# Pair pass of a graph network: edges cut on a fixed grid of 128-edge cells, first attribute stored turned, four PSUM banks for each product

## The chip, the cores and the metric

The kernel runs on one core of a Trainium2 chip. The time is device microseconds from launch to the last result; three runs gave 6835.71, 6841.29 and 6842.03 us, the median is 6841.29 us.

## The reference

A graph has 6250 nodes with 128 features and 106250 edges, sorted by target node. Four blocks are applied in turn: two attention layers, a normalised graph convolution, a block that uses attributes of each edge, and three graph convolutions. The change is about the third block (`_L2_gnn_ref`), after a layer norm and a ReLU of the node features:

```
pos_e = x_feat[src] + edge_attr
v     = gelu(pos_e @ W1.T + b1) * bases
aggr  = segment_sum(v, dst)
```

`edge_attr` and `bases` are two inputs of 106250 x 128. The kernel uses that (x[src] + attr) W = (x W)[src] + attr W: the rows x W + b lie in a table in DRAM, and each edge needs one gathered row, one product of its attribute and one row of `bases`.

## The kernel before, in words

Nodes lie in 49 blocks of 128. A tile is 128 consecutive edges, taken to belong to one block; edges of a neighbour block in it are masked (their LOCAL number, the target's place in the block, is 128 or more, so no one-hot row has a one for them). There are 880 tiles, 220 groups of 4 (GT). Before, the first tile of a block starts at the block's first edge. `tile_tables` works out on VectorE the tables that say which block and which first edge each tile has, by a chain of small operations in which each waits for the one before. Then GpSimd fetches each tile's window of targets, sources and weights by indirect DMA, and VectorE makes LOCAL, SRC, KEY and others of them. Five passes use these tables. `sort_edges` counts whether any target is smaller than the one before; the counting sort runs only then, and these inputs are sorted.

`pair_pass` has one piece of code for each step of a group, and `pipeline` writes them out for step u = 0, 1, 2, ... with a distance ("late"): a piece with distance d works on group u - d. Every engine runs its own pieces in that order. Before, for group q:

- `gather_rows` (distance 0, GpSimd, line 1033): 4 indirect DMAs, each bringing 128 rows of the table into one of 12 group slots (DEEP); it waits until group q - 12 is summed.
- `fetch` (0, SyncE, L1643 to L1657): loads the 4 tiles' first edges into registers, branches on sorted or not, and issues 4 loads of 128 x 256 (attribute and base side by side, 128 KB) into one of 6 slots (PD).
- `turn_attr` (1, TensorE, L1666): 4 transposes of the attribute into PSUM.
- `copy_attr` (1, ScalarE, L1673): PSUM to SBUF. It waits for `attr_turned` and `pre_done` alone.
- `times_w` (2, TensorE, L1681): 4 products with the weight into one of two banks `pre`.
- `sum_up` (2, VectorE, L1690): adds the gathered rows; it waits for the product, the gathers and a slot of V.
- `gelu` (2, ScalarE, L1694), `times_base` (3, VectorE, L1700).
- `hots` (2, VectorE, L1045): 4 one-hot matrices.
- `products` (4, TensorE, L1714): 4 products that sum the edges by target, into one of two banks `sums`.
- `add` (5, VectorE, L1063): 4 additions to the blocks' accumulators, each waiting for the one before.

`into_pair_pass` ahead of it stores the table, so no gather can start earlier; `two_norms` after it starts behind a barrier. Two attention passes (the L1033 rows with ACC) and the three last convolutions (L1348) also gather through GpSimd.

## Time and profile before

| | |
|---|---|
| median of the runs | 6841.29 us |
| span of the profiled execution | 8166.8 us |
| mean granted TensorE clock in it | 0.779 of full |
| pair pass, first to last gather issued | 5108.4 to 6471.1 us |
| GpSimd busy over the span | 57% |
| TensorE busy over the span | 74% |

The page gives no time of the profiled execution beside its span; that span is 1325.5 us above the median of the runs, so durations and gaps below are of an execution that was a fifth longer than a run. A row of the trace says how often an instruction came, how long one took, and what ended the idle time before it on its engine. The name behind a DMA releaser is a guess where several transfers share a semaphore.

### The profile page before, as it was taken

The numbers are of one execution on the slowest core, as the hardware profiler recorded it, in microseconds if no ns is written. First come the engines' busy times: TensorE is split into PE (matmuls) and PEld (weight loads), VectorE is DVE, ScalarE is ACT, GpSimd is POOL, SyncE is SP. The second block draws the span as 40 slices with busy tenths as digits, with TensorE's granted clock in tenths as the row PEclk, the third lists the DMA queues.
The fourth block names the chain that finished last, engine by engine and source line by source line (L and its number), as shares of the span: only waits on it lengthen the run. The fifth ranks groups of instructions, "written<-read, shape, count | busy, mean of one in ns | idle before, by whom it ended". The sixth has DMA issues, their size and how long they took to land. (4 is left out here: it accounts for less than half of the span.)

```text
span 8166.8 us, 113382 instructions
## 1 busy us (share of the span) xinstructions
PE 6013.4 (74%) x30494; PEld 4713.9 (58%) x30494; DVE 3761.8 (46%) x13003; ACT 2160.8 (26%) x7007; POOL 4622.4 (57%) x4391
## 2 busy tenths in 40 slices
PE   3788878646766888876686887455555689989898
PEld 2666766535665666655575887355555544544545
DVE  5344443148973444311688335344555543333333
ACT  3222222228852222222697002111111220000000
POOL 2555555567865555555786552666666436366363
PEclk8666666768976666677898999677777789999999
DMA  5566654356642333323444664444444557867777
GB/s 202 180 188 207 206 177 130 109 93 142 140 78 69 79 77 80 73 61 60 63 76 73 238 228 154 116 128 126 127 128 127 107 178 261 291 230 265 262 263 239
DMA packets 904017, 1231.57 MB, mean 151 GB/s; under 512 B 230601, under 2 KB 640861, under 8 KB 890407
## 3 DMA queue, kind: packets, MB, share of 16 engines
q1 hardware_dynamic: 607544, 887.00, 34.1%
q0 software_dynamic: 207392, 219.55, 14.4%
q10 hardware_dynamic: 88428, 117.57, 4.2%
q8 instruction: 256, 4.19, 0.2%
q14 instruction: 397, 3.25, 0.1%
HBM read 987.45 MB, written 237.38 MB: 150 GB/s over the span
## 5 line engine op out<-in xcount | busy, mean ns | idle before, releaser
L1033 POOL DMA_INDIRECT ACC<-table,TABS x1760 | 1685.1, 957 | 1417.6 <-DMA kept<-ACC 814.0
L1348 POOL DMA_INDIRECT BUF<-table,TABS x840 | 795.3, 947 | 795.7 <-DMA table<-ACC 258.1
L1033 POOL DMA_INDIRECT BUF<-table,TABS x880 | 872.7, 992 | 554.4 <-issue 258.4
L1114 POOL DMA_INDIRECT adjacency<-TABS x600 | 966.9, 1611 | 303.2 <-issue 265.7
L1807 PE MATMUL picked<-ident,ACC 128*128 128x128 f32 (+1 forms) x3520 | 967.5, 364 | 156.7 <-issue 155.4
L1827 PE MATMUL lcol<-attT,BUF 128*128 128x8 f32 (+1 forms) x3520 | 619.6, 299 | 314.7 <-ACT BUF L1845 248.2
L1827 PEld LDWEIGHTS lcol<-attT,BUF 128*128 128x128 f32 (+1 forms) x3520 | 611.6, 259 | 399.1 <-issue 397.1
L1807 PEld LDWEIGHTS picked<-ident,ACC 128*128 128x128 f32 (+1 forms) x3520 | 727.4, 237 | 186.9 <-issue 186.8
L1806 PE MATMUL picked<-G,OH 128*128 128x128 f32 (+1 forms) x2352 | 680.0, 379 | 193.3 <-issue 178.6
L1819 DVE TENSOR_TENSOR BUF<-BUF,picked 128x512 f32<-128x512 f32 (+1 forms) x440 | 298.5, 679 | 1072.5 <-ACT BUF L1813 843.0
L1806 PEld LDWEIGHTS picked<-G,OH 128*128 128x128 f32 (+1 forms) x2352 | 472.9, 237 | 383.2 <-issue 362.9
L2187 PE MATMUL asum<-BUF 128*128 128x144 f32 x3520 | 558.2, 304 | 166.3 <-DVE BUF L2165 125.6
L1833 ACT ACTIVATE ACC<-lcol 128x32 f32<-128x32 f32 (+1 forms) x440 | 81.2, 184 | 1989.1 <-DMA table<-BUF 788.2
L2187 PEld LDWEIGHTS asum<-BUF 128*128 128x128 f32 x3520 | 474.0, 196 | 197.2 <-issue 190.4
L1714 PE MATMUL sums<-BUF,G 128*128 128x128 f32 x1760 | 345.0, 358 | 325.4 <-DVE ACC L1063 243.6
L1883 DVE SCALAR_TENSOR_TENSOR BUF<-BUF,TABS,wspread 128x128 bf16<-128x128 f32 (+1 forms) x600 | 324.3, 541 | 529.9 <-issue 225.5
L2133 ACT ACTIVATE BUF<-iota_row,TABS 128x128 f32<-128x128 f32 x1760 | 555.2, 386 | 23.4 <-PEq L89 23.4
L1681 PE MATMUL pre<-wmat,BUF 128*128 128x128 f32 x1760 | 328.5, 347 | 249.4 <-ACT BUF L1673 246.6
L1714 PEld LDWEIGHTS sums<-BUF,G 128*128 128x128 f32 x1760 | 304.1, 260 | 357.7 <-issue 357.1
L1063 DVE TENSOR_TENSOR ACC<-ACC,asum 128x144 f32 (+1 forms) x1760 | 462.3, 263 | 92.4 <-issue 11.7
L1262 PE MATMUL sums<-ACC,BUF 128*128 128x128 f32 x3332 | 428.9, 290 | 65.1 <-issue 36.0
L1262 PEld LDWEIGHTS sums<-ACC,BUF 128*128 128x128 f32 x3332 | 414.9, 205 | 75.5 <-issue 61.5
(397 smaller groups left out, 10236.7 us busy)
## 6 DMA issues: line engine op xcount, KB each, us to landing
TABS<-adjacency SPq DMA_DIRECT2D x272, 512.0 KB
BUF<-in_edge_pair SPq DMA_DIRECT2D x880, 128.0 KB
BUF<-adjacency SPq DMA_DIRECT2D x102, 1024.0 KB
BUF<-adjacency SPq DMA_DIRECT2D x204, 512.0 KB
adjacency<-zeros ACTq DMA_DIRECT2D x44, 1792.0 KB
G<-adjacency SPq DMA_DIRECT2D x136, 512.0 KB
kept<-ACC SPq DMA_DIRECT2D x220, 272.0 KB
G<-kept SPq DMA_DIRECT2D x220, 272.0 KB
```

The lines of the kernel that those rows point to most:

```text
L1033: po.indirect_dma_start(rows[:, slot, j, 0:width], None, tab, bass.IndirectOffsetOnAxis(ap=SRC[:, q * GT + j:q * GT + j + 1], axis=0)).the ...
L1063: ve.tensor_tensor(at, at, self.from_[:, j, 0:self.width], ALU.add).then_inc(S("added"), 1)
L1114: po.indirect_dma_start(adj_flat, bass.IndirectOffsetOnAxis(ap=PLACE[:, k:k + 1], axis=0), TOTAL[:, k:k + 1], None, compute_op=ALU.add).th ...
L1262: m = pe.matmul(sums[:, j, 0:P], RA[n % len(RA)][:, (i * w + j) * P:(i * w + j + 1) * P], xw[:, b + i, :], start=b + i == 0, stop=b + i == ...
L1348: po.indirect_dma_start(R[:, q % deep_ring, j, :], None, table, bass.IndirectOffsetOnAxis(ap=SRC[:, k:k + 1], axis=0)).then_inc(S(f"gather ...
L1681: m = pe.matmul(pre[h][:, j, :], EAT[:, h, j, :], wmat[:, :], start=True, stop=True)
L1714: m = pe.matmul(sums[h][:, j, :], HOTS[:, slot, j, :], V[:, q % 4, j, :], start=True, stop=True)
L1806: pe.matmul(z, XRB[q % 3][:, j, :], OHT[:, slot, j, :], start=True, stop=False)
L1807: m = pe.matmul(z, R[:, q % DEEP, j, :], ident[:, :], start=False, stop=True)
L1827: m = pe.matmul(lcol[slot % 2][:, j * H:(j + 1) * H], Z[:, q % 3, j * P:(j + 1) * P], attT[0:W, 0:H], start=True, stop=True)
L2133: ac.activation(HOT[:, slot, j, :], iota_row[:, :], ACT.Abs, scale=-1.0, bias=LOCAL[:, bass.ds(q * GT + j, 1)]).then_inc(S("gap"), 1)
L2187: m = pe.matmul(sums[slot % 2][:, j, 0:WIDE], HOT[:, slot, j, :], RHS[:, slot, j, :], start=True, stop=True)
```

## The change

The 128-edge tiles are cut on a fixed grid: cell c holds edges 128 c to 128 c + 127. A block's tiles are all cells that hold one of its edges, so a cell on a border of two blocks is a tile of both; edges below the block are masked too (LOCAL negative). 831 cells and 48 borders give at most 879 tiles; the number of tiles and groups is still 880 and 220, and so are the sizes of the parts that other passes use. The host stores the attribute of each cell turned (its 128 x 128 transposed) beside the base, so the transposes on TensorE and the copies on ScalarE go. `pre` and `sums` have four PSUM banks each (before two, and two for `turned`), V and the one-hots 6 slots (4), the pair loads 9 slots (6). SyncE branches once, and issues all loads in the branch taken. Distances: product 1, sum and gelu 4, base and one-hots 5, product by target 6, addition 9.

```
-NEAR_TILES = LIGHT * (E + CYCLE * (P - 1)) // (CYCLE * P)
+NEAR_TILES = LIGHT * (SORT_T + CYCLE - 1) // CYCLE
...  tile_tables
-            go(ve, lambda: ve.tensor_tensor(number[:, 0:NB], starts[:, 1:NB + 1], starts_t, ALU.subtract))
-            go(ve, lambda: ve.tensor_scalar(number[:, 0:NB], number[:, 0:NB], float(P - 1), None, ALU.add))
-            go(ve, lambda: ve.tensor_copy(number_i, number[:, 0:NB]))
-            go(ve, lambda: ve.tensor_scalar(number_i, number_i, 7, None, ALU.logical_shift_right))
-            go(ve, lambda: ve.tensor_copy(number[:, 0:NB], number_i))
+            def first_cell(cell, edges, plus):
+                go(ve, lambda: ve.tensor_scalar(number_i, edges, float(plus), None, ALU.add))
+                go(ve, lambda: ve.tensor_scalar(number_i, number_i, 7, None, ALU.logical_shift_right))
+                go(ve, lambda: ve.tensor_copy(cell, number_i))
+            first_cell(first, starts_t, 0)
+            first_cell(shift, starts[:, 1:NB + 1], P - 1)
+            go(ve, lambda: ve.tensor_tensor(shift, shift, first, ALU.subtract))
+            go(ve, lambda: ve.tensor_tensor(filled, starts[:, 1:NB + 1], starts_t, ALU.is_gt))
+            go(ve, lambda: ve.tensor_tensor(number[:, 0:NB], shift, filled, ALU.mult))
...
-            go(ve, lambda: ve.scalar_tensor_tensor(shift, first, float(-P), starts_t, ALU.mult, ALU.add))
+            first_cell(shift, starts_t, 0)
+            go(ve, lambda: ve.tensor_tensor(shift, shift, first, ALU.subtract))
+            go(ve, lambda: ve.tensor_scalar(shift, shift, float(P), None, ALU.mult))
...
+            go(ve, lambda: ve.tensor_scalar(cell, edge, 1.0 / P, None, ALU.mult))
...
-            go(ve, lambda: ve.tensor_scalar(real_edge, local, float(P), None, ALU.is_lt))
+            go(ve, lambda: ve.tensor_scalar(real_edge, local, 0.0, None, ALU.is_ge))
+            go(ve, lambda: ve.scalar_tensor_tensor(real_edge, local, float(P), real_edge, ALU.is_lt, ALU.mult))
...  pair_pass
-            PD = 6
+            PD, VD, FREE = 9, 6, 4
+            SUM_LATE, BASE_LATE, PRODUCT_LATE, ADD_LATE = 4, 5, 6, 9
...
-                turned = [psum(ps, f"turned{i}", [P, GT, P]) for i in range(2)]
-                pre = [psum(ps, f"pre{i}", [P, GT, P]) for i in range(2)]
-                sums = [psum(ps, f"sums{i}", [P, GT, P]) for i in range(2)]
+                pre = [psum(ps, f"pre{i}", [P, GT, P]) for i in range(FREE)]
+                sums = [psum(ps, f"sums{i}", [P, GT, P]) for i in range(FREE)]
...
-                            sp.dma_start(PAIR[:, q % PD, j, :], pairs[bass.ds(at[j], P), :]
+                            sp.dma_start(PAIR[q % PD][:, j, :], cells[bass.ds(at[j], 1), :, :].rearrange("a p d -> p (a d)")
...
-                        m = pe.transpose(turned[h][:, j, :], PAIR[:, q % PD, j, 0:D], ident[:, :])
-                    ac.activation(EAT[:, h], turned[h][:, :, :], ACT.Copy).then_inc(S("attr_copied"), 1)
-                    wait(pe, S("summed"), q - 1)
+                    wait(pe, S("summed"), q - FREE + 1)
-                        m = pe.matmul(pre[h][:, j, :], EAT[:, h, j, :], wmat[:, :], start=True, stop=True)
+                        m = pe.matmul(pre[q % FREE][:, j, :], PAIR[q % PD][:, j, 0:D], wmat[:, :], start=True, stop=True)
-                    wait(pe, S("added"), (q - 1) * GT)
+                    wait(pe, S("added"), (q - FREE + 1) * GT)
...
-                pipeline(nc, [(gather_rows, 0), (fetch, 0), (turn_attr, 1), (copy_attr, 1),
-                              (times_w, 2), (times_base, 3), (sum_up, 2), (gelu, 2), (hots, 2), (products, 4),
-                              (add, 5)])
+                with sp.If(unsorted == 1):
+                    fetch_all(pair_s)
+                with sp.Else():
+                    fetch_all(A["edge_pair"])
+                pipeline(nc, [(gather_rows, 0), (times_w, 1), (add, ADD_LATE), (times_base, BASE_LATE), (hots, BASE_LATE),
+                              (sum_up, SUM_LATE), (gelu, SUM_LATE), (products, PRODUCT_LATE)])
...  gat_logits, put_aside (once in each attention layer)
+                    ve.scalar_tensor_tensor(LATER[:, cols], LOCAL[:, cols], 0.0, LATER[:, cols],
+                                            ALU.is_lt, ALU.add).then_inc(S("aside"), 1)
...  kernel, on the host
-    inputs["edge_pair"] = np.concatenate([inputs.pop("edge_attr_128"), inputs.pop("edge_attr_128_n2")], axis=1)
+    attr, base = (np.pad(np.asarray(inputs.pop(name)), ((0, CELLS * P - E), (0, 0))).reshape(CELLS, P, D)
+                  for name in ("edge_attr_128", "edge_attr_128_n2"))
+    inputs["edge_pair"] = np.concatenate([attr.transpose(0, 2, 1), base], axis=2).reshape(CELLS * P, 2 * D)
```

Left out are the sort (which turns the attribute tile by tile, and is not run on these inputs), its loop counts and the padding of the copies.

TensorE in the middle of the pass, two groups before; pool7 counts copied attributes, pool1 sums, pool16 additions, pool3 base products, pool13 one-hots, pool5 and pool6 pair loads:

```order
L1681 MATMUL pre_67<-wmat,BUF 128x128 [waits pool1,pool7]
L1681 MATMUL pre_67<-wmat,BUF 128x128 x3
L1714 MATMUL sums_69<-BUF,G 128x128 [waits pool16,pool3,pool13]
L1714 MATMUL sums_69<-BUF,G 128x128 x3
L1666 MATMUL turned_65<-ident,BUF 128x128 [waits pool7,pool5]
L1666 MATMUL turned_65<-ident,BUF 128x128 x3
L1681 MATMUL pre_68<-wmat,BUF 128x128 [waits pool1,pool7]
L1681 MATMUL pre_68<-wmat,BUF 128x128 x3
```

The same place now; pool12 counts sums, pool18 additions, pool1 base products, pool17 one-hots, pool7 to pool9 pair loads:

```order
L1686 MATMUL pre_67<-wmat,BUF 128x128 [waits pool12,pool7]
L1686 MATMUL pre_67<-wmat,BUF 128x128 x3
L1717 MATMUL sums_70<-BUF,OH 128x128 [waits pool18,pool1,pool17]
L1717 MATMUL sums_70<-BUF,OH 128x128 x3
L1686 MATMUL pre_68<-wmat,BUF 128x128 [waits pool12,pool8]
L1686 MATMUL pre_68<-wmat,BUF 128x128 x3
```

Four transposes a group are gone, and a product with the weight waits for its load and for a bank, for no ScalarE copy.

VectorE in the same pass, one group before; pool16 is the additions' own count, pool12 gelu, pool11 the products by target, pool9 the products with the weight, pool15 a pair load:

```order
L1063 TENSOR_TENSOR ACC<-ACC,sums_69 128x128
L1700 TENSOR_TENSOR BUF<-BUF 128x512 [waits pool15,pool12]
L1690 TENSOR_TENSOR BUF<-pre_68,BUF 128x512 [waits pool11,gathered5_91735,pool9]
L1045 TENSOR_SCALAR G<-iota_row,TABS 128x128 [waits pool11]
L1045 TENSOR_SCALAR G<-iota_row,TABS 128x128 x3
L1017 TENSOR_LOAD BLOCK [waits pool11]
```

And now (pool16 is gelu here, pool15 the products by target, pool14 those with the weight, pool7 a pair load; lines 1704, 1070, 1694 and 1042 are the former 1700, 1045, 1690 and 1017):

```order
L1726 TENSOR_TENSOR ACC<-ACC,sums_71 128x128
L1704 TENSOR_TENSOR BUF<-BUF 128x512 [waits pool7,pool16]
L1070 TENSOR_SCALAR OH<-iota_row,TABS 128x128 [waits pool15]
L1070 TENSOR_SCALAR OH<-iota_row,TABS 128x128 x3
L1694 TENSOR_TENSOR BUF<-pre_68,BUF 128x512 [waits pool15,gathered11_105377,pool14]
L1042 TENSOR_LOAD BLOCK [waits pool15]
```

The sum, which waits for the gathers, now stands behind the one-hots, last in its step. VectorE's instructions for a group are the same ten.

## Rows read from the trace of the kernel before

**Rows 1.** Span and mean granted TensorE clock:
```profile
core 0: 8166.8 us, clock 0.779
```
**Rows 2.** The page's costliest groups: the lines that gather through GpSimd:
```profile
L1033 POOL DMA_INDIRECT ACC<-table,TABS x1760 | 1685.1, 957 | 1417.6 <-DMA kept<-ACC 814.0
L1348 POOL DMA_INDIRECT BUF<-table,TABS x840 | 795.3, 947 | 795.7 <-DMA table<-ACC 258.1
L1033 POOL DMA_INDIRECT BUF<-table,TABS x880 | 872.7, 992 | 554.4 <-issue 258.4
```
**Rows 3.** Groups by form, 5140 to 6500 us: busy, mean ns, idle, releasers:
```profile
L1033 POOL DMA_INDIRECT BUF<-table,TABS x855 | 848.8, 993 | 483.7 <-issue 251.1 <-DVE BUF L1690 232.6
L1714 PE MATMUL sums<-BUF,G 128*128 128x128 f32 x1712 | 336.4, 358 | 318.6 <-DVE ACC L1063 236.7 <-issue 81.6
...
L1063 DVE TENSOR_TENSOR ACC<-ACC,sums 128x128 f32 x852 | 242.4, 285 | 92.9 <-issue 1.9 <-DVE ACC L1063 0.7
L1045 DVE TENSOR_SCALAR G<-iota_row,TABS 128x128 f32<-128x128 f32 x860 | 192.6, 291 | 0.0
L1666 PE MATMUL turned<-ident,BUF 128*128 128x128 f32 x860 | 176.5, 344 | 37.7 <-DMA BUF<-in_edge_pair 37.6
L1690 DVE TENSOR_TENSOR BUF<-pre,BUF 128x512 f32<-128x512 f32 x215 | 148.0, 689 | 612.1 <-DMA BUF<-adjacency 460.8 <-PE pre L1681 123.5 <-issue 27.7
L1700 DVE TENSOR_TENSOR BUF<-BUF 128x512 f32<-128x512 f32 x215 | 147.2, 685 | 0.7 <-issue 0.7
...
L1673 ACT ACTIVATE BUF<-turned 128x512 f32<-128x512 f32 x215 | 127.1, 591 | 565.6 <-DMA BUF<-adjacency 473.4 <-issue 71.1 <-PE turned L1666 21.2
```
**Rows 4.** Windows, all of the pass's middle: length, busy by engine, clock, DMA share, GB/s:
```profile
5140.00:6500.00 1360.00, 758.35 (x4292) 702.39 (x4293) 665.56 (x2142) 255.54 (x430) 848.65 (x855) 0.72 0.46 126
```
**Rows 5.** Line 1033 in this pass: ns min/median/max, first and last start:
```profile
L1033 POOL DMA_INDIRECT BUF<-table,TABS x880: 939/946/1467, 5108.4 to 6471.1; - x176
```
**Rows 6.** Timeline, one standstill: start us, us, instruction, idle before and releaser:
```profile
5782.32 0.60 PE L1666 MATMUL turned<-ident,BUF 128*128 128x128 f32 x4
...
5782.76 1.06 PE L1681 MATMUL pre<-wmat,BUF 128*128 128x128 f32 x8
...
5792.50 0.60 ACT L1673 ACTIVATE BUF<-turned 128x512 f32<-128x512 f32 x1 [8.62 <-DMA BUF<-adjacency]
5792.59 0.69 DVE L1690 TENSOR_TENSOR BUF<-pre,BUF 128x512 f32<-128x512 f32 x1 [6.51 <-DMA BUF<-adjacency]
...
5794.07 0.95 POOL L1033 DMA_INDIRECT BUF<-table,TABS  x1 [3.41 <-DVE BUF L1690]
```
**Rows 7.** Line 1652, SyncE's own instructions: ns min/median/max:
```profile
L1652 SPq FUSED_REGOPS  x880: 2/37/1396, 5112.7 to 6495.4; - x176
L1652 SPq MOVE BUF<-in_edge_pair x880: 2/29/1400, 5112.8 to 6495.4; - x176
```
**Rows 8.** Timeline of TensorE at its lower clock:
```profile
5777.03 2.04 PE L1714 MATMUL sums<-BUF,G 128*128 128x128 f32 x8 [0.54 <-DVE ACC L1063]
5778.87 1.06 PE L1666 MATMUL turned<-ident,BUF 128*128 128x128 f32 x4
5779.72 1.87 PE L1681 MATMUL pre<-wmat,BUF 128*128 128x128 f32 x8
5781.43 0.83 PE L1714 MATMUL sums<-BUF,G 128*128 128x128 f32 x6
```
**Rows 9.** Timeline near the end, all gathers issued, two sums running:
```profile
6486.51 0.68 DVE L1690 TENSOR_TENSOR BUF<-pre,BUF 128x512 f32<-128x512 f32 x1
...
6489.98 0.68 DVE L1690 TENSOR_TENSOR BUF<-pre,BUF 128x512 f32<-128x512 f32 x1
```
**Rows 10.** Timeline of VectorE while the tables are made:
```profile
48.79 0.21 DVE L504 TENSOR_TENSOR st<-st 128x49 f32<-128x49 f32 x1 [1.99 <-PEq L345]
49.03 0.19 DVE L505 TENSOR_SCALAR st<-st 128x49 f32<-128x49 f32 x1
...
56.53 0.52 DVE L521 TENSOR_TENSOR BUF<-st 128x343 f32<-128x343 f32 x1
...
93.70 0.63 DVE L595 CAST BUF<-BUF 128x910 f32<-128x910 int32 x1 [10.93 <-DMA BUF<-w_sorted,st]
...
107.00 1.09 DVE L619 SCALAR_TENSOR_TENSOR BUF<-BUF 128x896 f32<-128x896 f32 x1
```

More of the change, by code:

```diff
@@ L25 @@
 FRONT = P
-TAIL = 2 * P
+TAIL = 4 * P
 GT = 4
@@ L555, in tile_tables @@
                 rows = psum(ps, "rows", [1, 2, 1024])
-                for n, (col, tab) in enumerate(((blk, BLOCK), (edge, START))):
+                for n, (col, tab) in enumerate(((blk, BLOCK), (cell, START))):
                     for g in range(TCOL):
@@ L1640, in gather_rows, with fetch_all @@
                     gather(table, R, D, q, lambda: wait(po, S("summed"), q - DEEP + 1))
-                def fetch(q, slot, turn):
-                    at = nc.values_load_multi_w_load_instructions(
-                        START[0:1, bass.ds(q * GT, GT)], engines=(SP,), min_val=0, max_val=E,
-                        skip_runtime_bounds_check_because="a tile's first edge is a minimum with E")[1]
-                    wait(sp, S("based"), q - PD + 1)
-                    settle(sp, "sync")
-                    def rows(pairs):
+                def fetch_all(pairs):
+                    cells = pairs.rearrange("(c p) d -> c p d", p=P)
+                    for q in range(GROUPS):
+                        at = nc.values_load_multi_w_load_instructions(
+                            START[0:1, bass.ds(q * GT, GT)], engines=(SP,), min_val=0, max_val=CELLS - 1,
+                            skip_runtime_bounds_check_because="a tile's cell is a minimum with the last one")[1]
+                        wait(sp, S("based"), q - PD + 1)
+                        settle(sp, "sync")
@@ L1682, in times_w @@
                     m.then_inc(S("pre_done"), 1)
                 def sum_up(q, slot, turn):
[L1685 removed]
                     ve.wait_ge(S("pre_done"), q + 1)
                     gathered(ve, q)
[L1689 to L1690 removed]
+                    wait(ve, S("v_free"), q - VD + 1)
+                    ve.tensor_tensor(V[:, q % VD], pre[q % FREE][:, :, :], R[:, q % DEEP], ALU.add).then_inc(S("summed"), 1)
@@ L1713, in products @@
                     for j in range(GT):
-                        m = pe.matmul(sums[h][:, j, :], HOTS[:, slot, j, :], V[:, q % 4, j, :], start=True, stop=True)
+                        m = pe.matmul(sums[q % FREE][:, j, :], HOTS[q % VD][:, j, :], V[:, q % VD, j, :], start=True, stop=True)
                     m.then_inc(S("v_free"), 1)
                 def add(q, slot, turn):
-                    adder.start(q, slot)
+                    ve.wait_ge(S("v_free"), q + 1)
+                    blocks = blocks_of(DVE, q)
@@ L1719, in add @@
                     for j in range(GT):
-                        adder.tile(j)
+                        wait(ve, S("added"), q * GT + j)
+                        at = acc[:, bass.ds(blocks[j], 1), :].rearrange("p a d -> p (a d)")
+                        ve.tensor_tensor(at, at, sums[q % FREE][:, j, :], ALU.add).then_inc(S("added"), 1)
                 def load_ahead():
```

71 lines of the change are left out of this document (33 added, 38 removed).

## The prediction

> **What bounds the kernel now.** I read the span first [rows 1]: 8166.8 us, where the median of the runs is 6841.29 us. The profiled execution is 1325.5 us longer than a run, so its busy times may be carried over and its waits only with care. The page gives no time around the span; I set every sum against 8166.8 us for the profile and then ask what of it a run can hold.
>
> The costliest groups [rows 2] show three passes that gather 880 groups' tiles through GpSimd: two of attention (1760 gathers with ACC) and the pair pass (880 with BUF). By form over the pair pass's middle [rows 3], GpSimd has 848.8 us busy and 251.1 us of "issue" for 855 gathers, which is 1.286 us from one to the next where nothing else holds it, 5.15 us a group of four. The first and last gather lie 1362.7 us apart [rows 5]; 880 x 1.286 = 1132 us. The rest, 231 us, is the 232.6 us that GpSimd waits for line 1690, the sum that frees a slot.
>
> What works behind the gathers is shorter. VectorE has (242.4 + 192.6 + 148.0 + 147.2) / 215 = 3.40 us a group [rows 3]. When all gathers had been issued, two sums followed each other at 3.47 us [rows 9]. TensorE at its lower clock goes from one group's products to the next in 5781.43 - 5777.03 = 4.40 us, transposes included [rows 8]. ScalarE has under 1.3 us. DMA is 46% busy [rows 4]. So the middle of the pass has one pace that nothing behind it reaches: 5.15 us of GpSimd.
>
> Why then does the trace show 6.2 us a group? The timeline of a standstill [rows 6]: the transposes started at 5782.32, the product at 5782.76, both short. ScalarE's copy, which waits in the code for TensorE alone, starts at 5792.50; the sum at 5792.59. The page names a DMA for both, but the copy waits for none: its real releaser is TensorE's count, about 9.5 us after the 0.60 us that the row gives to the transposes. In the same pass SyncE's register moves, which wait for nothing, have a median of 29 ns and a longest of 1400 ns [rows 7]. Something that is neither data, bank nor slot holds several sequencers at once. Since the runs are 1325.5 us shorter, I take it that these standstills belong mostly to the profiled execution. Two numbers support that. GpSimd's waits for others in the three passes add up to 814.0 + 232.6 = 1047 us [rows 2, 3], near the difference. And if the pass shrank as the whole did (6841.29 / 8166.8 = 0.838), it would take 1362.7 x 0.838 = 1142 us, 10 us above GpSimd's own 1132 us. In the runs, then, the pair pass already goes at the pace of its gathers, with 12 groups of slots to smooth what is behind.
>
> **The change part by part.**
>
> Transposes and copies: 880 transposes at 344 ns (303 us of TensorE) and 220 copies at 591 ns (130 us of ScalarE) go [rows 3]. All of it lies beside the gathers: TensorE falls from 4.40 to about 3.55 us a group (less 5779.72 - 5778.87 = 0.85 us [rows 8]), VectorE stays at 3.40 to 3.47 us, both under 5.15 us. If that cover were gone (gathers quicker than 1.10 us), the most that is saved is what TensorE gives back, 220 x 0.85 = 187 us. I take nothing for it.
>
> Four banks and longer distances: they take away TensorE's waits for additions (236.7 us [rows 3]), again beside the gathers. The sum still waits for its own gathers and frees the slot as before; it stands last in its step, but in a pass paced by gathers the additions, base product and one-hots ahead of it are done while it waits. Between nothing and the whole 231 us, I take 0 to 10 us, by the 1142 us above: 5 us.
>
> Pair loads: as many, of 128 KB, from rows of 1 KB as before; SyncE loses one branch a group. Nine slots instead of six put more of them in flight at the start; at 46% DMA share [rows 4] I take nothing. The bound above nothing is in the slower rival.
>
> The drain: after the last gather lands, VectorE had a sum, the one-hots, an addition group, the base product and three addition groups; now it has the sum, one addition group, the base product, the one-hots and four addition groups, so one addition group more. What is left of 3.47 us [rows 9] less the sum (0.69), the base product (0.68) and the one-hots (0.90) [rows 3] is 1.2 us for such a group: +1.2 us. Nothing else runs there, so this is on the path.
>
> The tables: ahead of the window gathers the chain has 9 operations where it had 5, and further on 5 where it had 1, each 0.24 us after the last (49.03 - 48.79 [rows 10]): 8 x 0.24 = +1.9 us on the path, since the windows are what VectorE waits for at 93.70 (10.93 us idle). The cell's number lies inside that wait: nothing. The second operation for real_edge is one like line 619, 1.09 us: +1.1 us, in a chain in which each waits for the last. LATER gets one more operation in each attention layer, on 320 or 280 columns; line 521 with 343 columns took 0.52 us: at most 2 x 0.5 = +1.0 us, if GpSimd waits for it.
>
> Tiles and groups stay 880 and 220, and so does every other pass's count, so I carry nothing for them.
>
> Sum: +1.9 + 1.1 + 1.0 + 1.2 = +5.2 us, less 5 us: +0.2 us. On the median: 6841.3 + 0.2, rounded up, 6842 us. Against the profiled execution the sum is another: if its standstills stayed as they are, 8167 us; if the shorter code behind the gathers avoids them all, 8166.8 + 5.2 - 231 = 7941 us. I expect its span between these two, and its fall to be no measure of the runs.
>
> **The rivals.**
>
> A. In the runs the gathers are quicker than the trace shows. Their busy time alone is 945 ns [rows 5], 3.78 us a group; the 0.29 us between two is issue time that a run may not have in full. Then TensorE at its lower clock (4.40 us) paces the pass before, and the gathers or VectorE after: up to (4.40 - 3.78) x 220 = 136 us. For it speaks that the clock was 0.72 in the pass [rows 4]; against it that a denser TensorE gets its full clock, at which the pace before is VectorE's 3.47 us and the gain nothing. From 1.10 us a gather upward it is nothing too. Middle: 6842 - 75 = 6767 us.
>
> B. The standstills are in the runs too, as bubbles that come of having two banks and short distances. Then four banks and longer distances take the gathers to their own pace: -231 us at most, 6611 us; half of it gives 6842 - 116 = 6726 us, and I take the half as its centre, since the 1325.5 us must come from somewhere. Against it stands the copy that starts 10 us late with free slots and its transposes issued [rows 6], and the register moves [rows 7].
>
> The Trainium skill, Perfetto Trace Analysis, section Optimization Strategy, says that the same gap repeating for a stretch can mean too little SBUF or PSUM for the next tile, and its section Matmul Optimizations asks for all eight banks. By that rule this change should bring rival B's gain; the rows on SyncE's moves speak against it here, and it has no more weight than B's chance.
>
> C. Slower: the gathers get longer. Most last 946 ns, some up to 1467 ns, mean 993 ns [rows 3, 5]: about one in ten is long. If nine loads in flight and the denser use of SBUF doubled the share of long ones, each gather would cost 47 ns more, 880 x 47 ns = 41 us, all on the path, as GpSimd is the pace: 6842 + 41 = 6883 us. It decides from +16 ns a gather (14 us). For it: the path has no slack there, so any delay counts. Against it: the bytes are the same.
>
> D. The change does not do what it says, for instance a load or a bank waits in its place. The rows of the order show products that wait for a load and the sum three groups back, with nine slots; I give it nothing of its own.
>
> **How the numbers follow.** A measurement of this kernel tells 0.2% (about 14 us) from no change. The forecast, within 0.2%, has 0.47. A has 0.15, B 0.21, and both count as faster: 0.36. C has 0.17. The likeliest's own range is 6828 to 6855 us. The range reaches over A whole, over B to its centre, and over most of C: 6725 to 6875 us. That leaves out about half of B (0.1) and the far part of C (0.07).
>
> **What would show it.** Lines 1666 and 1673 have no successor, and TensorE's weight products wait for loads. If I am right, the gathers' start to start stays at 1.25 to 1.30 us, GpSimd's wait for the sum falls from 232.6 us or stays, the profile's pass shortens by up to 231 us, and the median does not move. A median more than 14 us lower with gathers at the same spacing proves B, and that the standstills are no matter of the profiled execution. A lower one with gathers closer than 1.25 us speaks for A. A mean gather above 1009 ns at no lower wait is C. The tables' chain should put the first attention gather some 1.9 to 3 us later.

## The result, and the profile after

The changed kernel takes 11216.15 us (median of 4 runs, 11144.81 to 11319.13), the kernel before 6838.5 us (4 runs, 6830.28 to 6842.03): 1.6382 times as long, 95% interval 1.6338 to 1.6426. The ratio is taken without the longest of the changed kernel's four runs. The forecast was 6842 us. The profiled execution of the changed kernel took 11167.97 us with a span of 11166.2 us.

The page of the changed kernel shows at once where it went. In the 40 slices of the span, 15 hold almost no compute, and a 16th only a little:

```profile
span 11166.2 us, 110756 instructions
...
PE   0000000000000001899847799868796555599999
...
DVE  1000000000000002555279655338645665644444
ACT  0000000000000001333449433339502111200000
POOL 0000000000000000777778677778674777564755
PEclk9999999999999999677869777779898767799999
DMA  2222222222222224888557444334585555389998
...
q1 hardware_dynamic: 821044, 887.00, 34.5%
...
L520 DVE TENSOR_SCALAR st<-st 128x49 int32<-128x49 f32 x3 | 0.6, 190 | 4303.7 <-PEq L347 4303.6
```

VectorE idles 4303.7 us ahead of line 520, the first operation on the tables, while the DMA engines are a quarter busy and move nothing worth counting. The queue q1 has 821,044 packets with the same 887.00 MB as before; before it had 607,544. That the page puts the wait down to TensorE's sequencer at line 347 is only where the control flow joins: every engine waits there for SyncE. SyncE's own timeline names the work (start us, us, instruction):

```profile
5.43 0.73 SPq L233 DMA_DIRECT2D BUF<-in_dst  x2
6.21 0.81 SPq L303 DMA_DIRECT2D src_sorted<-in_src  x1
7.06 2108.50 SPq L303 DMA_DIRECT2D dst_sorted<-in_dst  x1
2115.61 0.68 SPq L303 DMA_DIRECT2D w_sorted<-in_edge_weight  x1
2116.34 2231.94 SPq L264 DMA_DIRECT2D adjacency<-zeros  x6
```

SyncE issues the copy of src in 0.81 us, is then held for 2108.50 us on the next DMA, issues the copy of the weights, and is held again for 2231.94 us. The slow transfers are the ones ahead of the two held issues: src and weights. Of the trace's four-byte packets 106,716 start before 2115.6 us and 106,886 between 2115.6 and 4348.3 us, one copy's in each wait. The transfers of one stretch of that time (packets, MB, share of 16 engines):

```profile
q1 hardware_dynamic: 51195, 0.20, 24.2%
```

That is 51,195 packets in 1000 us, four bytes each. The copies of src, dst and weights each hold one element for each of the 106250 edges and the tail, a padding behind them; the tail went from 2 x 128 to 4 x 128 elements. 106250 + 256 = 106506 = 9 x 11834, and the copy was issued as 9 pieces of 47,336 bytes. 106250 + 512 = 106762 = 2 x 53381, and 53381 is prime: a piece of 53381 elements is over 200 KB, and the copy falls into 106,762 pieces of one element. Twice that is 213,524; the queue has 213,500 more. dst has 128 elements more in front: 106890 = 15 x 7126, pieces of 28,504 bytes, and is quick.

The rest of the loss lies in the pair pass. Its own rows (line 1058 is the old line 1033: duration ns minimum/median/maximum, first and last start; then the groups by line from 8560 to 9600 us; then the pass as one window, with the clock, the DMA share and GB/s at its end):

```profile
L1058 POOL DMA_INDIRECT BUF<-table,TABS x880: 941/947/1466, 8531.9 to 9701.7; - x176
...
L1058 POOL DMA_INDIRECT BUF<-table,TABS x781 | 802.9, 1028 | 238.1 <-issue 238.1
L1694 DVE TENSOR_TENSOR BUF<-pre,BUF 128x512 f32<-128x512 f32 x196 | 135.5, 691 | 328.2 <-issue 324.5 <-DMA BUF<-table,TABS 3.7
L1704 DVE TENSOR_TENSOR BUF<-BUF 128x512 f32<-128x512 f32 x195 | 134.4, 689 | 0.3 <-issue 0.3
...
8531.00:9702.00 1171.00, 674.31 (x3504) 625.77 (x3504) 697.43 (x2170) 139.23 (x220) 902.06 (x880) 0.71 0.52 149
```

Against [rows 3, 5], GpSimd's wait for the sum is gone (232.6 us before), as are the transposes and copies, and the pass has shrunk from 1362.7 to 1169.8 us. But that is no gain in time, as the next kernel shows.

**The kernel before, once more (e3).** It was profiled a second time beside the first experiments and took 6813.79 us:

```profile
core 0: 6812.0 us, clock 0.846
...
L1033 POOL DMA_INDIRECT BUF<-table,TABS x880: 940/944/1456, 4231.3 to 5343.8; - x176
...
L1033 POOL DMA_INDIRECT BUF<-table,TABS x823 | 790.8, 961 | 251.0 <-issue 251.0
...
L1652 SPq FUSED_REGOPS  x880: 37/37/47, 4235.7 to 5324.0; - x176
L1652 SPq MOVE BUF<-in_edge_pair x880: 29/29/39, 4235.8 to 5324.1; - x176
```

None of SyncE's register operations at line 1652 lasts over 47 ns here, where [rows 7] had 1400 ns; GpSimd never waits for the sum in this pass, which takes 1112.5 us. So the fair comparison for the changed kernel's 1169.8 us is 1112.5 us, and the pass is 57.3 us longer. From the kernel before (e3) to the changed one the spans differ by 4354.2 us: 4306.2 until the first attention gather (4466.3 against 160.1 us), -5.6 from there to the pass, +57.3 in it, -3.7 behind its last gather.

### The profile page after: what moved, and what is told of

It is laid out like the page before. It is cut to its first block and busy times, and to the rows that moved or that the text cites. A ratio compares the mean times of both kernels' runs of the same rounds, so it can differ in the third digit from the quotient of the medians.

```text
span 11166.2 us, 110756 instructions
## 1 busy us (share of the span) xinstructions
PE 5443.9 (49%) x29614; PEld 4353.5 (39%) x29614; DVE 3798.7 (34%) x13015; ACT 2060.8 (18%) x6787; POOL 4672.4 (42%) x4391
## 3 DMA queue, kind: packets, MB, share of 16 engines
q1 hardware_dynamic: 821044, 887.00, 34.5%
## 5 line engine op out<-in xcount | busy, mean ns | idle before, releaser
L520 DVE TENSOR_SCALAR st<-st 128x49 int32<-128x49 f32 x3 | 0.6, 190 | 4303.7 <-PEq L347 4303.6
L1058 POOL DMA_INDIRECT BUF<-table,TABS x880 | 903.0, 1026 | 331.4 <-issue 331.4
L1373 POOL DMA_INDIRECT BUF<-table,TABS x840 | 799.9, 952 | 569.0 <-issue 247.1
L1816 PE MATMUL picked<-ident,ACC 128*128 128x128 f32 (+1 forms) x3520 | 887.3, 344 | 0.0
L1815 PE MATMUL picked<-G,OH 128*128 128x128 f32 (+1 forms) x2352 | 612.4, 352 | 176.1 <-DMA ACC<-table,TABS 99.5
L1816 PEld LDWEIGHTS picked<-ident,ACC 128*128 128x128 f32 (+1 forms) x3520 | 669.6, 221 | 0.0
L1686 PE MATMUL pre<-wmat,BUF 128*128 128x128 f32 x1760 | 363.3, 371 | 503.9 <-DVE BUF L1694 469.5
L1836 PEld LDWEIGHTS lcol<-attT,BUF 128*128 128x128 f32 (+1 forms) x3520 | 537.2, 232 | 55.3 <-issue 49.5
L1815 PEld LDWEIGHTS picked<-G,OH 128*128 128x128 f32 (+1 forms) x2352 | 427.0, 216 | 313.0 <-issue 285.4
L1836 PE MATMUL lcol<-attT,BUF 128*128 128x8 f32 (+1 forms) x3520 | 543.6, 277 | 2.7 <-ACT BUF L1854 2.7
L1686 PEld LDWEIGHTS pre<-wmat,BUF 128*128 128x128 f32 x1760 | 313.5, 268 | 551.7 <-issue 515.4
```

The lines of the kernel that those rows point to most:

```text
L1058: po.indirect_dma_start(rows[:, slot, j, 0:width], None, tab, bass.IndirectOffsetOnAxis(ap=SRC[:, q * GT + j:q * GT + j + 1], axis=0)).the ...
L1373: po.indirect_dma_start(R[:, q % deep_ring, j, :], None, table, bass.IndirectOffsetOnAxis(ap=SRC[:, k:k + 1], axis=0)).then_inc(S(f"gather ...
L1686: m = pe.matmul(pre[q % FREE][:, j, :], PAIR[q % PD][:, j, 0:D], wmat[:, :], start=True, stop=True)
L1815: pe.matmul(z, XRB[q % 3][:, j, :], OHT[:, slot, j, :], start=True, stop=False)
L1816: m = pe.matmul(z, R[:, q % DEEP, j, :], ident[:, :], start=False, stop=True)
L1836: m = pe.matmul(lcol[slot % 2][:, j * H:(j + 1) * H], Z[:, q % 3, j * P:(j + 1) * P], attT[0:W, 0:H], start=True, stop=True)
```

## The experiments

All times below come with the kernel before on the same chip. The runs of the first group had it at 6834.0 us, of the second at 6820.2, of the third at 6828.24, of the last at 6827.56 us.

**e1_after_502.** The changed kernel with `TAIL = 502` for `TAIL = 4 * P`: 106752 = 834 x 128.

> The changed kernel with one number changed: TAIL 502 for 512, so that the three copies ahead of the sort test have 106752, 106880 and 106752 elements (834 and 835 times 128) for 106762, 106890 and 106762. Theory 1 (padding): 106762 is 2 x 53381, a prime, and the copies of src and weight are cut into 4-byte pieces; with 502 the 4302 us gap ahead of the first table operation goes, and the time is 11216 less about 4302 = 6864 to 6914 us, or nearer to 6840 if my forecast for the rest was right. Theory 2 (the cells): the gap comes from something else that the change does to the start, such as the longer tables; then the time stays above 11000 us.

6854.88 us (12 runs), ratio 1.0038 [1.0022 to 1.0054]. The one number takes 4.36 ms away: VectorE's first table operation starts at 49.05 us. What is left of the change is a loss of 0.4%. By spans it is +33.2 us against e3: -2.6 up to the pass's first gather, +45.9 in the pass, -10.1 behind its last gather. The last two are taken up below.

```profile
L1058 POOL DMA_INDIRECT BUF<-table,TABS x880: 940/944/1520, 4228.7 to 5387.1; - x176
...
L1058 POOL DMA_INDIRECT BUF<-table,TABS x789 | 801.1, 1015 | 240.4 <-issue 240.4
```

**e2_before_512.** The kernel before with `TAIL = 4 * P` for `TAIL = 2 * P`, and nothing else of the change.

> The kernel before with TAIL 512 for 256 and nothing else. Theory 1: both copies fall into 4-byte pieces here too, two of about 2110 us one after the other, so 6840 + 4300 = 11140 us, with 213524 pieces more among the DMA packets. Theory 2: 6840 us.

11867.55 us, 728 us above the forecast. The issues behind the two copies take 2463 and 2590 us:

```profile
6.21 0.80 SPq L301 DMA_DIRECT2D src_sorted<-in_src  x1
7.06 2463.15 SPq L301 DMA_DIRECT2D dst_sorted<-in_dst  x1
2470.25 0.67 SPq L301 DMA_DIRECT2D w_sorted<-in_edge_weight  x1
2470.97 2590.49 SPq L262 DMA_DIRECT2D adjacency<-zeros  x1
```

Cells, turned attributes and banks have no part in the 4.3 ms. What a copy in single elements costs is not one number: the same two copies take 713 us more here than in the changed kernel, at 44 packets a us where that had 51.

**e3_before_again.** The kernel before, unchanged.

> The kernel before, unchanged, profiled once more. If the standstills in its first trace (span 8166.8 us) belong to that one execution, this span is near 6840 us, SyncE's register moves have a longest of some 30 to 50 ns for 1400 ns, and the pair pass runs from first to last gather in 1130 to 1180 us. If they belong to the kernel, the span is above 8000 us again.

6813.79 us; its rows stand above. The standstills of [rows 6, 7] are not in it.

**e4_weight_split.** The changed kernel, weights copied in two pieces:

```
-for copy, given in ((src_s, A["src"]), (dst_s, A["dst"]), (w_s, A["edge_weight"])):
+for copy, given in ((src_s, A["src"]), (dst_s, A["dst"]), (w_s[0:E], A["edge_weight"][0:E]),
+                    (w_s[E:E + TAIL], A["edge_weight"][E:E + TAIL])):
```

> The changed kernel with TAIL 512, and only the weight's copy issued as two (106250 elements and 512). 106250 is 2 x 5^5 x 17 and cuts into large pieces. Theory 1: the source's copy alone stays in 4-byte pieces, so one half of the gap goes: 11216 - 2150 = about 9060 us, with 106762 small packets fewer. If the two slow copies ran beside each other and not one after the other, it would stay near 11200 us.

9485.51 us, about 425 us above the forecast: one of the two waits is gone, and the other is 2646.72 us long, at 42 packets a us. Why the pace of the pieces differs between these runs isn't shown. The bytes are the same; the shape of one copy decides.

**e13_tail_484.** The changed kernel with `TAIL = 484`: 106734 = 6 x 17789.

> The changed kernel as it is but for the tail: 484 elements instead of 512, so src and the weights have 106734 = 6 x 17789 elements (512: 2 x 53381, both factors beyond it prime) and dst, with 128 more, stays well divisible (7 x 15266). Theory (each piece that a copy is cut into costs about the same time; 512 added 213,500 packets on SyncE's queue and 4301.6 us): pieces of 24 bytes, so about 35,600 more packets on that queue than in e1, and VectorE's first operation on the tables at 650 to 850 us instead of 4350. Rival (any number of elements without a large divisor costs the same): it stays near 4350 us. Rival 2 (time goes by the bytes): it is at 50 us as in e1.

8885.44 us. The count of pieces was forecast wrongly: q1 has 820,994 packets, 213,412 more than e1 and twice 106,734 but for some 60, so they are single elements here too, not 24 bytes. Yet the wait is about half: line 520 starts at 2084.81 us instead of 4350.42, which neither the theory nor one of its rivals had.

```profile
7.20 947.65 SPq L303 DMA_DIRECT2D dst_sorted<-in_dst  x1
954.89 0.76 SPq L303 DMA_DIRECT2D w_sorted<-in_edge_weight  x1
955.69 1126.98 SPq L264 DMA_DIRECT2D adjacency<-zeros  x6
...
q1 hardware_dynamic: 71587, 0.29, 63.2%
```

The last row is of 300 to 900 us: 119 packets a us at 63.2% of the engines, where the tail of 512 had 51 at 24.2%. So the price isn't that of a packet alone: more of the engines' time is in use at once, 10.1 of 16 engines by the share where it was 3.9. The Trainium skill, DMA: Bandwidth & Descriptors, section Why a DMA increments its semaphore by 16 and not by 1, states both halves: a contiguous row of over 64 KiB whose element count has no divisor that fits a descriptor becomes one descriptor per element if software cuts it into equal pieces, and a copy goes to the largest number of engines, at most 16, that divides its outer dimension on both sides. The packets agree; of the engines the direction agrees (2 and 6 by the rule), but three times the engines gave 2.2 and 2.0 times the pace here, and up to 2.8 times against the slower copies of e2 and e4. No run counts the engines themselves, so that the factor in front of the prime sets the pace rests on two lengths and the page.

**Second question: 46 us in the pass.** In e3, e1 and the changed kernel GpSimd leaves 0.305 us between two gathers and waits for nobody, so a pass is 879 times (mean gather + 0.305 us): with 0.961 it is 1112.5, with 1.013 it is 1158.4 us. Most gathers last 944 ns; what differs is how many are long. The timeline of e1 shows a normal round and a long one (start us, us):

```profile
4803.92 0.69 DVE L1704 TENSOR_TENSOR BUF<-BUF 128x512 f32<-128x512 f32 x1
4804.21 1.21 POOL L1058 DMA_INDIRECT BUF<-table,TABS  x1 [0.30 <-issue]
...
4807.34 0.69 DVE L1694 TENSOR_TENSOR BUF<-pre,BUF 128x512 f32<-128x512 f32 x1 [1.86 <-issue]
4807.95 1.56 DVE L1726 TENSOR_TENSOR ACC<-ACC,sums 128x128 f32 x4
4808.22 0.94 POOL L1058 DMA_INDIRECT BUF<-table,TABS  x1 [0.30 <-issue]
```

The gather at 4804.21 starts 0.29 us into line 1704, the base product, and lasts 1.21 us; the one at 4808.22 starts in line 1726 and lasts 0.94. Over the pass, 148 of 880 gathers last over 1.1 us, and all of them start 0.04 to 0.4 us after a base product does; 145 are the fourth of their group. In e3 32 do. In the first trace of the kernel before, from which [rows 3] are, it is 101, at the same place: the cause stood there before the forecast. The product is the one VectorE operation of the pass with both operands in SBUF. In e3 VectorE's round is product, sum, one-hots, additions, and the product stands mostly between two gathers' starts:

```profile
4802.67 0.69 DVE L1700 TENSOR_TENSOR BUF<-BUF 128x512 f32<-128x512 f32 x1
4802.90 1.13 PE L1714 MATMUL sums<-BUF,G 128*128 128x128 f32 x8 [0.83 <-DVE ACC L1063]
4803.48 0.94 POOL L1033 DMA_INDIRECT BUF<-table,TABS  x1 [0.30 <-issue]
```

In the changed kernel's round (sum, additions, product, one-hots) it comes 0.8 us earlier behind the sum (2.09 us after its start, in e3 2.88). The sum starts when its gathers land, so the round is locked to GpSimd's, and the product meets the start of the group's fourth gather again and again.

**e5_base_last.** e1 with two pieces of one list exchanged:

```
-(add, ADD_LATE), (times_base, BASE_LATE), (hots, BASE_LATE),
+(add, ADD_LATE), (hots, BASE_LATE), (times_base, BASE_LATE),
```

> The changed kernel with the tail of 502 elements, and in the list of the pair pass's pieces the one-hots stand before the base product, so that VectorE goes sum, additions, one-hots, base product as in the kernel before (there: base product, sum, one-hots, additions). Theory 1 (collision: a gather whose start falls in the first 0.4 us of the base product, the one VectorE operation of the pass with both operands in SBUF, is held until that product ends; in the run e1 the product stood 2.1 us behind the sum, in phase with the fourth gather of nearly every sixth group): the product now starts about 2.9 us behind the sum, the long gathers (over 1.1 us) fall from 148 to under 50 of 880, the pass from 1158 to 1110 to 1120 us, and the kernel from 6854.9 to about 6812 (ratio to before 0.995 to 0.998). Rival (the long gathers come from the rows, the eager fetch of cells or the longer distances): the pass stays at 1155 to 1160 us and the ratio at 1.0035 to 1.004.

6801.2 us (10 runs), ratio 0.9978 [0.9967 to 0.9989]; 13 long gathers, pass 1107.5 us.

```profile
L1058 POOL DMA_INDIRECT BUF<-table,TABS x880: 940/944/1499, 4218.3 to 5325.8; - x176
...
L1058 POOL DMA_INDIRECT BUF<-table,TABS x827 | 789.2, 954 | 252.2 <-issue 252.2
```

The exchange turns the loss into a gain of 0.2%.

**e7_base_from_psum.** e1, the product's second operand in PSUM (the second attribute is left out of the result):

```
-ve.tensor_tensor(v, v, PAIR[q % PD][:, :, D:2 * D], ALU.mult)
+ve.tensor_tensor(v, v, pre[q % FREE][:, :, :], ALU.mult)
```

> The changed kernel with the tail of 502 elements, in which the base product multiplies by what lies in the group's PSUM bank instead of the second half of the pairs (this leaves the second attribute out of the result); the same size, place and engine, but one operand in SBUF instead of two, and TensorE's first product waits for the base product four groups back. Theory 1 (it is the two SBUF operands that hold a gather): long gathers (over 1.1 us) under 20 of 880, mean gather 950 to 965 ns, pass 1105 to 1120 us, span 6790 to 6815. Rival (any VectorE operation at that phase, or the gathered rows themselves): as e1, about 148 long ones, mean about 1015 ns, pass 1150 to 1160 us.

6793.66 us. Same place, same length, and no gather over 1097 ns, though 151 start in the first 0.4 us of a product (e1: 170); the pass takes 1102.0 us:

```profile
L1058 POOL DMA_INDIRECT BUF<-table,TABS x880: 940/944/1097, 4230.3 to 5332.3; - x176
```

This tells the operands from the place: a gather that starts under an operation with two SBUF operands is held for a part of what is left of it (the one above lasts 0.27 us more than 0.944, with 0.40 us of the product to go). The later it starts, the less it is held: in e1 the median is 1360 ns for starts 0.1 to 0.2 us into the product, then 1261, then 1163 ns for 0.3 to 0.4, and each of the 148 ends 1.50 to 1.59 us behind the product's start, all but a few at 1.50. Of the 22 that start in its first 0.04 us none is long. The Trainium skill, SBUF — State Buffer, section Who interferes with whom, says "A DVE instruction with two SBUF inputs contends with a GpSimd instruction that reads SBUF". The trace agrees for a gather whose row numbers lie in SBUF, with 148 gathers over 1.1 us in e1 and none in e7.

**e10_before_order.** The kernel before, with the additions and then the product ahead of the one-hots and the sum:

```
-(times_w, 2), (times_base, 3), (sum_up, 2), (gelu, 2), (hots, 2), (products, 4),
-(add, 5)])
+(times_w, 2), (add, 5), (times_base, 3), (hots, 2), (sum_up, 2), (gelu, 2),
+(products, 4)])
```

> The kernel before, with VectorE's round of the pair pass in the changed kernel's order: additions, base product, one-hots, sum (before: base product, sum, one-hots, additions); nothing else. Theory 1 (collision by the place of the base product): the long gathers rise from 32 to 120 to 180 of 880, the pass from 1112 to 1150 to 1165 us, the ratio to before is 1.004 to 1.008. Rival (it takes the change's cells or fetches as well): the pass stays within 1105 to 1125 us and the ratio within 0.998 to 1.002.

6841.53 us (10 runs; one of them took 20024.62 us at a mean granted clock of 0.241, for which nothing here has a reason), ratio 1.0021 [1.0009 to 1.0034]; 104 long gathers and a pass of 1129.8 us. The direction is as forecast, the size less than half: the collision can be put into the kernel before by the order alone, but 104 long ones are short of e1's 148, and what else of the change brings the product into phase isn't told apart.

**e6_two_banks.** e1 with `PD, VD, FREE = 9, 6, 2` and distances of 2, 3, 4 and 5.

> The changed kernel with the tail of 502 elements, with two banks a hop and distances of 2, 3, 4 and 5 groups for sum, base product, products and additions (e1: four banks, 4, 5, 6 and 9); the cells, the turned attribute and the order within VectorE's round stay. Theory 1 (collision, set by VectorE's order in its round): the product stands as far behind the sum as in e1, so the pass stays within 1140 to 1175 us and the ratio to before between 1.002 and 1.006. Rival (banks and distances matter, for better or worse): the pass leaves that range by 20 us or more; if the distances were what brought the long gathers, it is back at 1112.

6857.84 us, ratio 1.006 [1.0045 to 1.0074]; pass 1164.2 us. Banks and distances are worth nothing that these intervals tell from e1's 1.0038, and 5.8 us of the pass between two single profiles.

**e8_half_gathers_after, e9_half_gathers_before.** e1 and the kernel before, with two of a group's four gathers left out (`for j in range(2)` in `gather`, and the wait for it; half the rows of the table are missing from the result).

> The changed kernel with the tail of 502 elements, which gathers only the first two of a group's four tiles in the pair pass (the sums of the other two take what is left in the buffer, so the result is not the reference's). Theory 1 (GpSimd's gathers pace the pass): with 2.5 to 2.7 us of gathers a group the pass falls to what paces next, VectorE's 3.5 to 3.9 us a group with its waits: 770 to 880 us for 220 groups, and the span falls by 280 to 390 us from 6845. Rival (SP's fetches or the cells' transfers pace it): the pass stays above 950 us.

> The kernel before, which gathers only the first two of a group's four tiles in the pair pass (as e8 does of the changed kernel, whose gathers fell to 3.48 us a group and whose span was 6448.0). It tells what the change is worth once the gathers no longer pace the pass. Theory 1 (the change's banks, distances and fewer turnings lie beside the gathers, and are worth something only without them): TensorE's transposes, ScalarE's copy and the two banks now show, 3.6 to 4.2 us a group, so a span of 6480 to 6620, 30 to 170 above e8. Rival (VectorE's round of 3.5 us paces both): span within 20 us of e8's.

6449.83 and 6467.45 us. In both the sums follow each other at 3.47 us, which is VectorE's round without a wait. One window of 400 us of each, e8 first (PE, PEld, DVE, ACT, POOL busy):

```profile
4500.00:4900.00 400.00, 231.75 (x1835) 213.19 (x1833) 349.81 (x1149) 71.76 (x114) 217.64 (x230) 1.00 0.65 189
```
```profile
4500.00:4900.00 400.00, 282.32 (x2298) 263.76 (x2297) 349.61 (x1149) 127.86 (x230) 218.10 (x230) 1.00 0.65 190
```

The change takes 50.6 us from TensorE and 56.1 from ScalarE in this window, and none from VectorE. My theory for e9, that the change would be worth 30 to 170 us without the gathers' pace, fell: it is 18 us between two single profiles, and not in the pass, which takes 737.1 us in e8 and 735.6 us in e9; e9's starts 21.7 us later. Behind GpSimd stands VectorE, which the change leaves alone.

**e11_before_502.** The kernel before with `TAIL = 502`.

> The kernel before with a tail of 502 elements behind the copies of src, dst and weight (before: 256); nothing else. Theory 1 (the number of elements acts through its divisors alone; 106250 + 502 = 106752 = 834 x 128): ratio to before 0.998 to 1.002, VectorE's first operation on the tables at 48 to 51 us. Rival (a longer tail costs by itself, in the copies or in what waits for them): 1.002 or more, tables later by over 5 us.

6825.66 us, ratio 1.0 [0.9988 to 1.0013]. The longer tail itself is free, so e1 is the change without its accident.

**Third question: 10 us behind the last gather.** The forecast had the drain 1.2 us longer. From the last gather's start to the last addition's it takes 26.0 us in e3 and 14.3 in e1. The sums at the end of e3:

```profile
5348.94 0.69 DVE L1690 TENSOR_TENSOR BUF<-pre,BUF 128x512 f32<-128x512 f32 x1 [3.43 <-issue]
...
5355.70 0.69 DVE L1690 TENSOR_TENSOR BUF<-pre,BUF 128x512 f32<-128x512 f32 x1 [3.20 <-issue]
...
5360.80 0.69 DVE L1690 TENSOR_TENSOR BUF<-pre,BUF 128x512 f32<-128x512 f32 x1 [1.54 <-issue]
```

They stand 6.8 and 5.1 us apart, those ahead of them up to 8.2, and the last starts 17.0 us behind the start of its gather; in the middle of the pass it is 2.6 us. Meanwhile the gathers' queue keeps the engines busy with little data, e3 from 5330 to 5362 us, and e5 from 5312 to 5342 us:

```profile
q0 software_dynamic: 552, 1.12, 81.2%
```
```profile
q0 software_dynamic: 416, 0.85, 13.8%
```

By the sizes of the blocks, cells cut block by block fill 854 of the 880 tiles, and the fixed grid 879. The 26 empty tiles are the last six and a half groups, and all 128 lanes of such a tile gather row 0.

**e12_spread_rows, e15_spread_again.** The kernel before with values of src instead of zeros behind the last edge, so that the lanes of an empty tile gather different rows:

```
-a = np.pad(a, ((front, tail),) + ((0, 0),) * (a.ndim - 1), constant_values=fill)
+a = np.pad(a, pad, mode="wrap") if name == "src" else np.pad(a, pad, constant_values=fill)
```

> The kernel before, in which the 256 elements behind the last edge of src hold the first 256 values of src instead of zeros, so that the 128 lanes of an empty tile gather 128 different rows instead of one; their results carry no weight, and nothing else changes. By the sizes of the blocks 854 of the 880 tiles hold edges with the cells cut block by block, and 879 with the changed kernel's fixed grid: 26 empty tiles before, one after. Theory (gathers of one row by all lanes land late: in e3, the kernel before, the last seven sums of the pass stand 6.8 to 8.2 us apart and the last one 17.0 us behind its gather, in e5 4.0 us; it is where the changed kernel gains about 10 us behind its last gather): the last sums stand 5.0 to 5.3 us apart, the last addition ends 13 to 17 us behind the last gather instead of 26, and the ratio to before is 0.997 to 0.999. Rival (the late sums come from what SyncE or the distances do at the end of the pass): the last seven sums stay 6.7 us or more apart and the ratio stays within 0.999 to 1.001.

8157.84 us (12 runs), where the kernel before took 8171.91 us (17 runs, 8141.44 to 8183.28): ratio 0.9984 [0.9973 to 0.9995]. This chip is the kind of the first trace: GpSimd waits 240.5 us for the sum as in [rows 3], and SyncE's moves are as in [rows 7]:

```profile
L1652 SPq MOVE BUF<-in_edge_pair x880: 2/29/1393, 5105.4 to 6488.5; - x176
```

It tells nothing about empty tiles, since the sums lag by 69 us anyway, but it tells what the standstills are: of a chip (or its state then) and not of profiling alone, since each of the kernel before's 17 runs there is as long as the first trace, and e3, profiled on another chip, has none.

> The kernel of e12 once more (the kernel before, with 256 values of src instead of zeros behind the last edge, so that the lanes of its 26 empty tiles gather different rows), wanted on a chip on which the kernel before takes about 6830 us. Theory (one row gathered by all 128 lanes lands late): the last seven sums of the pass stand 5.0 to 5.3 us apart instead of 6.8 to 8.2, the last addition ends 13 to 17 us behind the last gather instead of 24 to 26, and the ratio to before is 0.997 to 0.999. Rival (the distances, or what SyncE does at the end of the pass): 24 to 26 us stay, and the ratio is 0.999 to 1.001. If the chip is again one of about 8170 us, it tells nothing.

6802.21 us, ratio 0.9963 [0.9948 to 0.9977], on another chip. The last sums stand 5.0 us apart but for the last (6.6), and the last addition starts 13.2 us behind the last gather. The second view is of the gathers' queue in the last 32 us, as for e3 above:

```profile
5345.17 0.69 DVE L1690 TENSOR_TENSOR BUF<-pre,BUF 128x512 f32<-128x512 f32 x1 [3.04 <-issue]
...
5352.94 1.58 DVE L1063 TENSOR_TENSOR ACC<-ACC,sums 128x128 f32 x4 [0.42 <-DVE ACC L1063]
```
```profile
q0 software_dynamic: 416, 0.85, 10.2%
```

So the drain's gain is the empty tiles'. The ratio is about 25 us, twice what the drain explains and beyond the theory's 0.997; where the rest lies isn't shown.

**e14_best.** e5 with the same values of src.

> The kernel of e5 (changed, tail 502, base product last in VectorE's round) with values of src behind the last edge as in e15. Theory (only empty tiles gain, and here 1 of 880 is empty): as e5, ratio to before 0.9965 to 0.999, the last addition 14 us behind the last gather. Rival (the other row values help elsewhere too): ratio under 0.9965.

6802.62 us, ratio 0.9968 [0.9953 to 0.9982], which its interval doesn't tell from e5's 0.9978, nor the theory from its rival. Versions of both kernels end near 6802 us (e5, e14, e15), 0.2 to 0.4% under the kernel before.

## Why the prediction was wrong, step by step

**The failed step: what the sum left out.** "Tiles and groups stay 880 and 220, and so does every other pass's count, so I carry nothing for them." The sum has a term for each line of the pair pass and of the tables, and none for the tail, `TAIL = 4 * P` for `2 * P`, the first line of the full diff, which the listing above leaves out with the padding. It adds 256 elements, 1 KB, to a copy, and I didn't factor the new length. Cost: two copies in single elements on the path, 4301.6 us later at the tables in the profiled execution, where the medians differ by 4377.7 (e1, e2, e4). No rival had it either, so even the range had nothing of the kind. The range has slips of its own: half of A's 136 us is 68 and not 75, A at its full size would be 6706 us, below the lower end of 6725 though the range is said to reach over A whole, and the upper end of 6875 us stops short of C's own centre, 6883.

**The gathers pace the pass: right.** 1.2656 us each in e3, forecast 1.286; in the pass of e3, e1 and e5 GpSimd waits for nobody, and with half the gathers the pass falls to 737 us (e8). **Transposes and copies are worth nothing: right**, and for a stronger reason than given: with half the gathers VectorE's 3.47 us pace both kernels (e8, e9). **Banks and distances: right in size** (0 to 10 us forecast; e5's pass is 5.0 us shorter than e3's, and four banks against two are 5.8 us in e1 against e6), but rival B's half and rival A hold nothing on the chips of the timings. The rule of the Trainium skill, Perfetto Trace Analysis, section Matmul Optimizations, that stood beside rival B (all eight banks, more room for the next tile) brought nothing that the runs tell from zero here, since what repeats is GpSimd's pace and no gap for want of a bank.

**Rival C was the one that came, by another mechanism.** It had +47 ns a gather and 41 us; e1 has +52 ns (0.961 to 1.013) and 45.9 us. The agreement is chance: I gave it to more loads in flight, with 0.17. It is the place of the base product in VectorE's round. The prediction used the new order of that round only for the drain and for what the sum leaves idle. [Rows 5] held the hint, a longest gather of 1467 ns with a median of 946 and 101 of 880 over 1.1 us in that trace, and I took the mean for a given instead of asking what the long ones had in common.

**The drain: wrong in sign**, -11.7 us (26.0 to 14.3) instead of +1.2. I counted VectorE's operations, while the last sums wait for gathers of empty tiles (e15), and the change fills those tiles. The count itself may stand: with the empty tiles out of the way the last addition starts 13.2 us behind the last gather in e15 and 14.3 in e1 and e5, 1.1 us more, though e14 has 12.9.

**The tables: right.** +1.9 and +1.1 us were forecast. The first attention gather starts at 163.2 to 165.0 us in the six kernels with the new tables and a tail of 502 (mean 163.8), and at 160.1 to 162.2 us in five with the old (e3, e9, e10, e11, e15: 160.8): +2.9 us. The two operations on LATER can't be seen apart.

**The standstills: half right.** They are not in the timed runs, as the sum assumed, so the span of 8166.8 us was rightly kept out of it. But they don't belong "to the profiled execution": on e12's chip each run is as long as if it had them. What the change does there wasn't tried.

## What to carry to other kernels

Factor every length that a change touches: a flat copy needs a divisor that gives pieces which one transfer takes (47,336 bytes went as one piece here, the 71,156 bytes of e13's sixths did not), and ten elements more or less were worth milliseconds here; the packets per queue and a DMA issue held for thousands of us show it. Where an engine sets the pace with operations of one kind, look at the distribution of their durations before the mean, and at what the long ones start under; the order within another engine's round then counts more than its work. And work that is hidden before a change stays worth nothing unless it is also the next in line when the pace is lifted.

## What the runs showed of the hardware that was not expected

- A copy of 417 KB in pieces of one element took 2108 to 2647 us with a factor of 2 in front of the prime (five copies) and 948 and 1127 us with a factor of 6, and held the issuing engine's next DMA for all of it (2108.50 us in the changed kernel).
- A gather of 128 rows that starts 0.04 to 0.4 us into a VectorE operation on two SBUF operands (0.69 us) lasted 1.1 to 1.5 us instead of 0.944 (148 in e1), and ended 1.50 us behind that operation's start, whenever it began; with one operand in PSUM none of 880 lasted over 1.1 us (e7).
- Gathers in which all 128 lanes read one row landed late: the sums of the last groups stand 5.1 to 8.2 us apart in e3, with 81.2% of the DMA engines' time for 1.12 MB in 32 us; with different rows it is 5.0 to 6.6 us and 10.2% (e15).
- The same program takes about 6830 us on some chips and 8172 us on another, with register moves of up to 1400 ns instead of 39.
